# State-space scan: a VectorE pair and two ScalarE instructions trade places, and one block diagonal changes engine

## What is computed

```python
def step(state, inp):
    dA_t, dtx_t, B_t, C_t = inp
    state = state * dA_t[..., None, None] + jnp.einsum('bgcp,bgn->bgcpn', dtx_t, B_t)
    y_t = jnp.einsum('bgn,bgcpn->bgcp', C_t, state)
    return (state, y_t)
...
y = jnp.moveaxis(ys, 0, 1) + D.reshape(1, 1, G, HPG, 1) * x
...
var = jnp.mean(jnp.square(yg), axis=-1, keepdims=True)
yn = (yg * lax.rsqrt(var + EPS)).reshape(b, l, INTER) * norm_w
out = yn * jax.nn.silu(z)
return out @ out_proj_w
```

## Time and profile before

| | |
|---|---|
| median of 3 runs | 511.39 us (511.18 to 514.34) |
| the profiled execution | 512.58 us, of which its span 510.70 us |
| TensorE busy, matmuls / weight loads | 470.6 / 396.2 us of the span |
| VectorE, ScalarE, GpSimd busy | 375.0, 280.0, 160.1 us |
| mean granted TensorE clock | 0.986 of full speed |

### The profile page before, as it was taken

How to read it: one execution, slowest core, us unless ns; L and a number is a source line. 1 busy time by engine, 2 the same in 40 slices (tenths; PEclk the granted TensorE clock), 3 DMA queues, 4 the chain that set the end, 5 groups by cost and what they waited for, 6 DMA issues and landing times.

```text
span 510.7 us, 17071 instructions
## 1 busy us (share of the span) xinstructions
PE 470.6 (92%) x7454; PEld 396.2 (78%) x7454; DVE 375.0 (73%) x745; ACT 280.0 (55%) x505; POOL 160.1 (31%) x215
## 2 busy tenths in 40 slices
PE   3979999999989999888899999999978999999997
PEld 3766798888888787766787788878857778898987
DVE  6977954656678999975788888888759766556443
ACT  3639644344327899998566656666545433323241
POOL 1010032203023111116666667667546310000000
PEclk9979999999999999899999999999989999999999
DMA  8940052000000000010000000000530000100001
GB/s 215 258 187 1 0 227 124 0 3 0 1 0 1 2 1 0 22 42 4 5 5 4 4 6 4 6 4 6 190 167 5 4 1 0 42 20 22 22 21 41
DMA packets 7226, 21.29 MB, mean 42 GB/s; under 512 B 752, under 2 KB 5360, under 8 KB 6512
## 3 DMA queue, kind: packets, MB, share of 16 engines
q1 hardware_dynamic: 6752, 18.05, 10.4%
q10 hardware_dynamic: 400, 2.16, 1.7%
HBM read 12.87 MB, written 6.55 MB: 38 GB/s over the span
## 4 chain that ended last, share of the span: by engine, by line
PE 37%; issue 7%; ACT 4%; POOL 3%; DVE 3%; POOLq 0%; DVEq 0%; ACTq 0%
PE intra L886 5%; PE seg L864 3%; PE yo L1008 2%; POOL w L1274 2%; PE seg L859 1%; PE XB L938 1%; PE new L989 1%; PE yo L954 1%; PE XB L974 1%; PE yo L1011 1%; PE prior L984 1%; PE XB L68 1%; PE yo L70 1%; PE yo L69 1%; PE yo L68 1%
## 5 line engine op out<-in xcount | busy, mean ns | idle before, releaser
L1274 POOL TENSOR_TENSOR w<-xdt,ends 32x512 f32<-32x512 f32 (+3 forms) x63 | 66.5, 1073 | 3.7 <-ACT seg L1035 2.3
L643 DVE SCALAR_TENSOR_TENSOR cv<-pre,vec,cv 128x512 f32<-128x512 f32 x72 | 52.9, 750 | 2.5 <-ACT cv L684 0.8
L514 POOL TENSOR_TENSOR n_rstd<-n_ve,m_half 128x4 f32<-128x4 f32 x12 | 13.0, 1086 | 125.7 <-DVE n_ve L509 125.6
L1035 ACT ACTIVATE seg<-seg 128x512 f32<-128x512 f32 x64 | 35.9, 579 | 29.2 <-PE seg L864 29.1
L1127 DVE TENSOR_TENSOR mmat<-seg,gs 128x512 f32<-128x512 f32 x64 | 42.4, 685 | 9.3 <-ACT seg L1035 8.9
L68 PE MATMUL pj<-n_xT,win 128*128 128x512 f32 x88 | 35.3, 401 | 4.8 <-ACT cv L684 2.4
L864 PEld LDWEIGHTS seg<-abk,m_seg 96*32 96x32 bf16 x2048 | 20.7, 96 | 24.2 <-DVE mmat L1127 13.7
L1048 ACT ACTIVATE f_hT<-f_h 128x512 fp32r<-128x512 f32 (+1 forms) x24 | 15.2, 632 | 40.2 <-DVE f_h L1138 40.2
L70 PE MATMUL pj<-n_xT,win 128*128 128x512 f32 x88 | 34.8, 395 | 0.0
L864 PE MATMUL seg<-abk,m_seg 96*32 96x64 bf16 x2048 | 27.0, 195 | 8.4 <-issue 5.6
L69 PE MATMUL pj<-n_xT,win 128*128 128x512 f32 x88 | 34.6, 393 | 0.0
(11 more groups left out here) (266 smaller groups left out, 1448.7 us busy)
## 6 DMA issues: line engine op xcount, KB each, us to landing
wgu_dram<-wgu SPq DMA_DIRECT2D x1, 2816.0 KB, 8.2
wgu<-wgu_dram SPq DMA_DIRECT2D x1, 2816.0 KB, 10.5
out<-x_res SPq DMA_DIRECT2D x8, 256.0 KB, 2.1
x_res<-in_x SPq DMA_DIRECT2D x1, 1536.0 KB, 22.5
wd_dram<-wd SPq DMA_DIRECT2D x1, 1536.0 KB, 11.6
wd<-wd_dram SPq DMA_DIRECT2D x1, 1536.0 KB, 13.6
gu_idx<-in_gu ACTq DMA_DIRECT2D x4, 352.0 KB, 8.3
gu_idx<-in_gu SPq DMA_DIRECT2D x4, 352.0 KB, 9.5
```

The source lines that it names most:

```text
L643: dve.scalar_tensor_tensor(dst, pre[:, x, k:k + GN].rearrange("p (t c) -> p t c", c=P), cw[:, x, k:k + 1], dst, ALU.mult, ALU.add).then_in ...
L1035: act.activation(seg[u_ % 2][:, :, :], seg[u_ % 2][:, :, :], ACT.Exp).then_inc(s["exp_ok"], 1)
L1274: pool.tensor_tensor(heads(w[r, n, :]), heads(xdt[a % 2][r, :]), ends[a % 2][r, n * HEADS:(n + 1) * HEADS].unsqueeze(2) .broadcast_to([Q * ...
```

## The change

Three things change, and no instruction is added or removed but for the engine of four:

1. VectorE's two `ssum` instructions move, in the 14 steps that have both an `a` and a `z`, from in front of `mmat` 1 and 2 to behind them. In the last two steps they stay where they were.
2. ScalarE's `uh<-u` moves in front of `sq<-yf`, in all 16 steps that have a `z`.
3. The block diagonal of block 1 is written by VectorE (four copies, right behind `xdt`) and no more by ScalarE.

```diff
--- before.py
+++ after.py
@@ -1081,16 +1081,16 @@
                 if z == LAST:
                     silu(0, 1)
                 if do_z:
-                    wait(act, "yf_ok", 4 * (z + 1))
-                    wait(act, "red_ok", z)
-                    act.activation(sq[:, :], yf[:, :], ACT.Square).then_inc(s["sq_ok"], 1)
                     wait(act, "u_ok", z + 1)
                     wait(act, "out_ok", z)
                     act.activation(uh[:, 0, :, :], u[:, :].rearrange("p (g t) -> p g t", g=4), ACT.Copy
                                    ).then_inc(s["uhi_ok"], 1)
+                    wait(act, "yf_ok", 4 * (z + 1))
+                    wait(act, "red_ok", z)
+                    act.activation(sq[:, :], yf[:, :], ACT.Square).then_inc(s["sq_ok"], 1)
                 if b_ == LAST:
                     norm.act_hi(act, 0)
-                if do_a and a:
+                if do_a and a > 1:
                     blocks_of_x(a)
                 if z == LAST:
                     act.wait_ge(hz, 1)
@@ -1142,6 +1142,14 @@
                 dve.tensor_tensor(low_part(hT, c, rows(c)), h[0:rows(c), :], hT[0:rows(c), 0, c, :].bitcast(F32),
                                   ALU.subtract).then_inc(h_lo, 1)
 
+            def sums_of_squares(z):
+                wait(dve, "sq_ok", z + 1)
+                wait(dve, "out_ok", z)
+                dve.tensor_tensor(ssum[:, :, :].rearrange("p a t -> p (a t)"), sq[:, 0:2 * P], sq[:, 2 * P:4 * P],
+                                  ALU.add).then_inc(s["half_ok"], 1)
+                wait(dve, "half_ok", z + 1)
+                dve.tensor_tensor(ssum[:, 0, :], ssum[:, 0, :], ssum[:, 1, :], ALU.add).then_inc(s["red_ok"], 1)
+
             norm.dve_start(dve)
             for a, b_, z, do_a, do_b, do_z in steps():
                 if do_a:
@@ -1151,12 +1159,13 @@
                     dve.tensor_tensor(heads(xdt[a % 2][:, :]), heads(XB[:, :]),
                                       T["dt_tok"][:, a, :].unsqueeze(2).broadcast_to([P, HEADS, PD]), ALU.mult
                                       ).then_inc(s["xdt_ok"], 1)
-                if a == 0:
+                if a < 2:
                     wait(dve, "set_ok", 2)
-                    wait(dve, "xdt_ok", 1)
+                    dve.wait_ge(T["blank"], 2)
+                    wait(dve, "xdt_ok", a + 1)
                     for b in range(NB):
                         r = slice(Q * b, Q * b + Q)
-                        dve.tensor_copy(xbd[0][r, :, b, :], heads(xdt[0][r, :])).then_inc(s["xbd_ok"], 1)
+                        dve.tensor_copy(xbd[a][r, :, b, :], heads(xdt[a][r, :])).then_inc(s["xbd_ok"], 1)
                 if do_z:
                     wait(dve, "ytr_ok", z + 1)
                     wait(dve, "sq_ok", z)
@@ -1173,12 +1182,8 @@
                     dve.tensor_tensor(u[:, :].rearrange("p (g t) -> p g t", g=4),
                                       yf[:, :].rearrange("p (g t) -> p g t", g=4),
                                       zs[:, z // GT, :, z % GT * P:z % GT * P + P], ALU.mult).then_inc(s["u_ok"], 1)
-                    wait(dve, "sq_ok", z + 1)
-                    wait(dve, "out_ok", z)
-                    dve.tensor_tensor(ssum[:, :, :].rearrange("p a t -> p (a t)"), sq[:, 0:2 * P], sq[:, 2 * P:4 * P],
-                                      ALU.add).then_inc(s["half_ok"], 1)
-                    wait(dve, "half_ok", z + 1)
-                    dve.tensor_tensor(ssum[:, 0, :], ssum[:, 0, :], ssum[:, 1, :], ALU.add).then_inc(s["red_ok"], 1)
+                if do_z and not do_a:
+                    sums_of_squares(z)
                 if b_ == LAST:
                     norm.dve_lo(dve, 0)
                 if z == LAST:
@@ -1197,6 +1202,8 @@
                     wait(dve, "intra_ok", a - 1)
                     masked(a, 1)
                     masked(a, 2)
+                if do_a and do_z:
+                    sums_of_squares(z)
                 blocks = lambda ap: ap.rearrange("p (b h d) -> p b h d", b=NB, d=PD)
                 if b_ == 0:
                     dve.memset(y[:, 0:P], 0.0).then_inc(s["t2_ok"], 1)
```

## The result

The changed kernel takes 518.12 us (median of 20 runs, 514.27 to 521.78) against 513.24 us of the kernel before beside it (20 runs, 511.18 to 517.98): a ratio of 1.0092, interval 1.0069 to 1.0116, some 4.7 us slower. Timed again beside fresh runs of the kernel before it was 1.0070, interval 1.0029 to 1.0111. The profiled execution took 518.02 us, its span is 516.2 (510.7 before).

The account below looks back on a forecast made before the run. TensorE bounds the middle steps, VectorE the end. Terms +0.9 - 0.8 + 0.54 + 0.84 + 0.48 + 1.9 = +3.9 us, put on the median 511.39, gave 515.3 us; range 510.0 to 518.5.

Parts of the forecast that it names:

- the third rival: VectorE and GpSimd turns last to the record's end, 0.15 us more at each of two turns; 517.6 us, chance 0.15.
- The collision: In loop steps, moved `ssum` meets GpSimd's `uh`, both `ssum` take about 1.1 us, `y<-XB` comes 1.4 us later.
- without a collision: Rival: `ssum` runs at its 0.43 us beside GpSimd, the loop gains 1.6 us; 510.4 us, chance 0.18.
- with the second `ssum` in front of `w`: Rival: second `ssum` slips ahead of GpSimd's `w`, `y<-XB` 0.5 us late, ring under 10; 512.2 us, chance 0.12.
- with GpSimd keeping its turn: Rival: VectorE gets in only behind both `w`, `y<-XB` begins at 315.8, ring 11.6 us; 527 us, chance 0.10.
- The gain at unit 3: Segments' unit 3: `mmat` 1 begins at the end of `u`, TensorE's waits go; 1.6 us by distances, blocks 3 to 14.
- Steps of no less than 10.4: Loop: VectorE's work per step, shorter by three waits, longer by 1.5 us blocking, takes 10.4 us; four shorter steps pay +0.9.
- `xdt` of block 15, +0.54: Before block 15's `xdt`, VectorE also does FFN statistics; `xdt`, for which TensorE waits already, comes 0.54 us later.
- `y` behind it, +0.84: Same step as block 15's `xdt`: `y`, for which TensorE waits already, comes 0.84 us later.
- Step of block 14's output, +0.48: `ssum` waits for GpSimd's low part of u, so TensorE's first FFN matmul goes from 405.19 to 405.67.
- The last step, +1.9: Later `sq` and the collision move `f_h` from 415.31 to 417.20; nothing absorbs it, +1.9 us.
- Idle stretches fixed to places: TensorE's idle stretches, some 10 us of the scan, taken as fixed to program places; 1 us either way.

Follow-up runs that it names:

- the PSUM version: Changed kernel, but in the loop's 14 steps both `ssum` take their second operand from PSUM (XB, maximum instead of sum); ratio 1.0051 to the kernel before.
- the swap alone: Kernel before with only ScalarE's `uh` put in front of `sq`, `ssum` staying in front of `mmat`; 552.34 us, ratio 1.0785.

## Why the prediction was right, and where its terms were off

Forecast was 515.3 us, +3.9 on a median of 511.39; the runs show +4.7 (+3.5 to +6.0) and, timed again, +3.6 (+1.5 to +5.7). Of the 2.8 us between 515.3 and 518.12, 1.85 are that the kernel before, too, was at 513.24 beside it. By its number alone 518.12 would speak for the third rival (turns to the end of the record, 517.6) rather than for the forecast; the rows speak against that one, as follows.

- **The collision: right, in place and size.** `ssum` at 1.07 and 1.06 us (about 1.1 forecast), `w` 0.23 longer (0.3), `y<-XB` 4.00 behind `u` (4.1), no wait before `x_res`. The rivals without a collision, with the second `ssum` in front of `w`, and with GpSimd keeping its turn are out by these rows alone: the order seen is `ssum`, `w`, `ssum`, `w`. VectorE's first `ssum` ends 0.27 us behind GpSimd's `uh`, at 313.40 against 313.13, and it is an instruction of 0.42 us by itself. So it began in earnest 0.15 us ahead of the other's end, as `u` did in the earlier trace rows, and `y<-XB` at 4.00 us leaves no room for two turns of 0.15 more, which is the third rival. The Trainium skill's page SBUF — State Buffer (Who interferes with whom) has the blocked side wait for the whole of the other instruction; the rows agree that the two take turns, and that only two operands in SBUF do it, but by the records the turn passes 0.15 us early. Records of neighbouring instructions overlap by some 0.07 us themselves, so this says where one may reckon the turn from, not when the chip gives it up.
- **The gain at unit 3: right.** All waits for `mmat` at L864 are gone.
- **"Steps of no less than 10.4": wrong.** After has steps of 9.82 and 9.85 us by TensorE's first transposes; from `u` to `u`, where VectorE's ring shows, the shortest are 10.19 to 10.23. Two things failed in this term. VectorE's ring without any wait is 10.20 us, not 10.4: in the second profile of the change `u` starts at 322.44 and again at 332.64 with no idle time between. And a ring is a floor only for a mean over steps: VectorE enters a short step with slack from the longer one before it, and TensorE's own step is 9.81 us, as `mmat` 1 ahead of `u` shows twice in a row. The +0.9 for four short steps was too much. The loop's balance, forecast at +0.1, can be had only as a difference: ratio times 513 less the end in the ledger, 4.7 - 4.2 = +0.5 for the one timing of the change, 3.6 - 4.2 = -0.6 for the other, the first with 1.2 us either way, the second with 2.1.
- **`xdt` of block 15, +0.54: mis-sized.** From the block's first XB matmul to `XB<-state` it is 4.18 us in both profiles before, 4.39 in one after and 4.18 in the other: 0 to +0.2. That VectorE had more slack there than the middle step shows would explain it, but no run tests this.
- **`y` behind it, +0.84: right**, +0.73 and +0.74.
- **Step of block 14's output, +0.48: mis-sized**, +1.11 and +1.18. The VectorE part is there, 0.55 us, when the clock stays up (the PSUM version). What was missed is that a wait of 2.1 us for `y` was followed by a stretch at half clock, which takes `XB<-state` from 1.08 to 1.94 us and `prior` from 0.84 to 1.51, and hides VectorE's part behind it.
- **The last step, +1.9: right**, 1.89 both times; and the swap is its cause, since the old order in the last two steps takes it back to the hundredth. The 0.5 us behind it, half clock again, had no term.
- **The start, nothing: right**, by the run with the copies alone.
- **"Idle stretches fixed to places": wrong in the main**, by the repeated profiles. The longest does keep its place, in the step in front of block 14, but not its length; the others keep neither. The forecast's 1 us either way for them was too narrow for one profile: 2.4 us between two profiles of one kernel.

Three of the end's terms don't follow to the hundredth from the figures beside them (1.4 - 0.8 is 0.6, 1.6 - 0.73 is 0.87, 404.26 + 0.67 + 0.69 is 405.62 and so +0.43), which comes to 0.04 us in all. They were +3.76 together, and +3.8 to +3.9 was measured for that stretch (the ledger's 3.73 and 3.78, and 0.21 and 0 for `xdt`), with 0.48 behind it. That the sum hit so well is in part luck, since errors cancel: the ring too dear by up to 0.9 us and `xdt` by 0.3 to 0.5, the clock left out at 0.6 and 0.5.

What stays open is what decides about the clock. In the last two steps there are eight waits of TensorE of 2.1 to 2.4 us: for `y` and for `f_h` in both profiles of the change, for `y` in those with the sums moved and with the last steps as before, for `f_h` in the PSUM version and in that of the swap alone. Six were followed by the half clock, the last two were not, and neither were the swap's waits of 2.59 us at 262 and 2.51 at 412. The kernel before has such a stretch as well, 0.50 behind the 3.29 us at 374. The clock's 0.5 us behind `f_h` is read from profiles with the same wait at either level; its 0.6 in the step before is a difference from the PSUM version, whose wait for `y` was shorter.

## What to carry to other kernels

Before moving a VectorE instruction with two SBUF operands, look at what GpSimd does at its new place; if the two meet, charge the rest of GpSimd's instruction, twice if the moved work is a pair. To feed a waiting engine earlier, move the short instruction that it waits for forward (one `mmat` ahead of `u`: -0.5%), not the ones in front of it backward. And charge a delay where its engine is the bound, at the end of a loop above all: `y<-XB` was 1.27 us later in the steps of the loop too, which came to no cost that the runs can tell from nothing (+0.5 and -0.6 us), and the last two steps cost 3.7 us. Last, before two profiles are subtracted, look for the step with the longest idle stretch: here one step, beside a large load, held all that one kernel's two profiles differed by.

## What the runs showed of the hardware that was not expected

- A VectorE operation of 128x256 with both operands in SBUF took 1.07 to 1.35 us beside GpSimd and 0.42 alone or with one operand in PSUM. Between two `w` that GpSimd has queued back to back a waiting VectorE instruction gets its turn.
- TensorE's granted clock fell to half behind waits of 2.13 and 2.41 us (changed kernel) and of 2.2 to 2.6 us (swap alone, ten steps in a row), there with 8 matmuls of `yo<-wout` at 2.08 us instead of 1.21, and not behind waits of 0.82, 1.19 and 1.35 us, nor behind four of 2.4 to 2.6. In two profiles (the copies alone, the PSUM operand) it fell behind 1.73 and 1.75 us at the scan's start, where in others the same wait left it at 1.00. Where it came in each step, a step was 1.0 to 1.1 us longer.
- One program's idle stretches without a releaser differ by 2.4 us between two executions, most of it in the one step beside the load of the weights, and the shorter ones stand at other places. So two whole profiles of these kernels can't be subtracted to better than that; a stretch without them can, to 0.06 us.
